# One semaphore of spent tiles in place of four bank counts behind the subtraction of row maxima

## What is computed

```python
# third attention (number 2 in the kernel): causal mask
scores = einsum('bhtd,bhsd->bhts', q, k) / sqrt(8) + causal
out = x + (softmax(scores) @ v) @ Wo.T + bo
# fourth attention (number 3): +1 outside a band of 16, then keep the 64 largest
scores = einsum('bhqd,bhkd->bhqk', q, k) * 8 ** -0.5 + outside
scores = where(scores >= kth, scores, 0)   # there are 64 keys, so all are kept
```

## Time and profile before

| | |
|---|---|
| median of 3 runs | 866.23 us |
| profiled execution | 868.9 us, its span (first to last instruction) 867.1 us |
| TensorE clock granted | 0.996 of full |
| TensorE matmul busy | 828.4 us (96%) in 7204 |
| VectorE busy | 630.4 us (73%) in 1587 |
| ScalarE busy | 567.4 us (65%) in 1569 |
| GpSimd busy | 286.4 us (33%) in 586 |
| attention 2, tiles 2 to 15 | 633 to 697 us |
| attention 3, tiles 0 to 15 | 745 to 833 us |

### The profile page before, as it was taken

How to read it: one execution, slowest core, us unless ns; L and a number is a source line. 1 busy time by engine, 2 the same in 40 slices (tenths; PEclk the granted TensorE clock), 3 DMA queues, 4 the chain that set the end, 5 groups by cost and what they waited for, 6 DMA issues and landing times.

```text
span 867.1 us, 20115 instructions
## 1 busy us (share of the span) xinstructions
PE 828.4 (96%) x7204; PEld 571.1 (66%) x7204; DVE 630.4 (73%) x1587; ACT 567.4 (65%) x1569; POOL 286.4 (33%) x586
## 2 busy tenths in 40 slices
PE   9999999999999999999999999999999989899986
PEld 8887888888889976544444444444467665676652
DVE  5677776777776655685785766775989876789876
ACT  3666677677777676866545586445477779677664
POOL 4355444444554442200000000002156520334355
PEclk9999999999999999999999999999999999999999
DMA  8700000000000000000000000000000000000000
GB/s 340 156 2 2 1 2 1 2 2 1 2 1 2 2 1 2 1 1 0 1 0 1 0 1 0 1 0 1 1 27 3 4 3 1 2 4 3 3 15 37
DMA packets 7821, 13.55 MB, mean 16 GB/s; under 512 B 4342, under 2 KB 5036, under 8 KB 7468
## 3 DMA queue, kind: packets, MB, share of 16 engines
q1 hardware_dynamic: 7724, 12.27, 4.5%
HBM read 11.22 MB, written 1.05 MB: 14 GB/s over the span
## 4 chain that ended last, share of the span: by engine, by line
PE 59%; DVE 20%; POOL 10%; issue 6%; ACT 4%; DMA 0%; DVEq 0%; POOLq 0%; SPq 0%; ACTq 0%
PE psum L1551 10%; PE psum L767 6%; POOL rstd L515 4%; PE psum L807 4%; DVE arena L2083 3%; PE psum L750 3%; PE psum L759 3%; POOL arena L1095 2%; DVE negmax L1005 2%; PE psum L835 2%; PE psum L1560 2%; PE psum L1978 2%; ACT arena L905 2%; PE psum L2367 2%; PE psum L1570 2%
## 5 line engine op out<-in xcount | busy, mean ns | idle before, releaser
L512 POOL TENSOR_TENSOR ve<-mv,epsv 128x1 f32<-128x1 f32 x176 | 36.3, 206 | 462.1 <-DVE mv L507 462.1
L1551 PE MATMUL psum<-arena,w1f 128*128 128x512 f32 x240 | 109.5, 592 | 0.0
L515 POOL TENSOR_TENSOR rstd<-ve,epsv 128x1 f32<-128x1 f32 x176 | 101.2, 575 | 13.8
L905 ACT ACTIVATE arena<-psum,negmax 128x128 f32<-128x128 f32 x256 | 90.5, 407 | 22.2 <-DVE negmax L1005 22.2
L1551 PEld LDWEIGHTS psum<-arena,w1f 128*128 128x128 f32 x240 | 45.5, 190 | 49.9 <-issue 46.1
L1095 POOL TENSOR_TENSOR arena<-arena,rsum 128x512 f32<-128x512 f32 x64 | 65.2, 1039 | 5.6 <-DVE rsum L1011 5.6
L905 ACT ACTIVATION_READ_ACCUMULATOR arena<-psum,negmax 128x1 f32 x256 | 63.2, 247 | 0.0
L1005 DVE TENSOR_REDUCE negmax<-psum 128x8 f32<-128x1024 f32 x32 | 39.2, 1225 | 32.9 <-PE psum L807 32.9
L750 PE MATMUL psum<-arena,sclA 128*128 128x128 f32 x512 | 62.5, 275 | 0.1
L767 PE MATMUL psum<-arena 128*128 128x512 f32 x128 | 61.2, 598 | 0.7 <-DVE arena L1000 0.4
L807 PE MATMUL psum<-arena 128*128 128x128 f32 x512 | 59.9, 275 | 0.0
(11 more groups left out here) (371 smaller groups left out, 1995.7 us busy)
## 6 DMA issues: line engine op xcount, KB each, us to landing
w<-in_w0qk SPq DMA_DIRECT2D x2, 512.0 KB, 4.6
w<-in_w0vo SPq DMA_DIRECT2D x1, 1024.0 KB, 7.3
cT<-in_cT SPq DMA_DIRECT2D x1, 1024.0 KB, 16.7
out<-x_tok SPq DMA_DIRECT2D x4, 256.0 KB, 2.2
rows<-in_rows SPq DMA_DIRECT2D x1, 836.0 KB, 12.3
x_tok<-in_x_tok SPq DMA_DIRECT2D x1, 768.0 KB, 9.4
ctx_tok<-in_ctx_tok SPq DMA_DIRECT2D x1, 768.0 KB, 10.8
wa<-in_wa SPq DMA_DIRECT2D x1, 768.0 KB, 18.5
```

The costliest lines, as they stand in the source:

```text
L515: pool.tensor_tensor(rstd[:, u, self.i:self.i + 1], ve[:, u, self.i:self.i + 1], epsv[:, 1:2], ALU.pow) \
L905: m = nc.scalar.activation(e0[:, b, g, :], ps(k, P, j * P), ACT.Exp, bias=negmax0[:, b, g:g + 1], accum_out=sum0[:, b, g:g + 1])
L1551: nc.tensor.matmul(ps(k), w1("e2", j * 384 + arg * D, j * 384 + (arg + 1) * D), f1_Hm[:, n, 2 * j + i, :], start=False, stop=False)
```

## The change

Each of the two attentions gets one semaphore `spent`, which the subtraction raises on completion. TensorE's four mask matmuls wait for `spent >= t` instead of each for its own bank (tile 0 still waits for the banks, which other jobs held before). ScalarE's exponential has one wait in place of four. VectorE's wait and three increments behind each subtraction go; at tile 15 VectorE waits once and raises all four banks by 16, so that the plan's counts hold for the jobs behind.

```diff
-            spread, maxed, exped, inverted = (sem(f"a{n}_{x}") for x in ("spread", "max", "exp", "rsum"))
+            spread, maxed, exped, inverted, spent = (sem(f"a{n}_{x}") for x in ("spread", "max", "exp", "rsum", "spent"))
...
-                        fill(pe, a, f"s{i}", t)
+                        if t.n == 0:
+                            fill(pe, a, f"s{i}", t)
+                        else:
+                            pe.wait_ge(spent, t.n)
...
-                    for i in range(4):
-                        stored(act, a, f"s{i}", t)
+                    act.wait_ge(spent, t.times(1, 1))
...
-                        .then_inc(free[0], 1)
-                    stored(dve, a, "s0", t)
-                    for i in range(1, 4):
-                        dve.sem_inc(free[i], 1)
+                        .then_inc(spent, 1)
+                    if t.n == TILES - 1:
+                        dve.wait_ge(spent, TILES)
+                        for i in range(4):
+                            dve.sem_inc(free[i], TILES)
```

## The result

The changed kernel takes 863.4 us (median of 20 runs, 860.44 to 866.58) against 866.76 us (20 runs, 865.67 to 868.94) for the kernel before, measured beside each other: ratio 0.9956, interval 0.9946 to 0.9966. Measured again in a pair of 8 and 27 runs it gave 863.66 against 867.77, ratio 0.9940 (0.9917 to 0.9963). The forecast was 861.6 us, in a range of 859.6 to 865.0, and faster. (Of the partner runs of the kernel before, one took 949.4 us at a granted clock of 0.85; it is left out everywhere.)

The account below looks back on a forecast made before the run. No engine's busy share decides: attention 2 loops through TensorE, attention 3 through VectorE's gap, barely above a TensorE-ScalarE cycle. Terms 0.4 + 2.2 + 1.05 + 1.2 - 0.2 = 4.65 us, from 866.23 to 861.6; range 859.6 to 865.0.

Parts of the forecast that it names:

- the forecast's own case: Whole kernel: gain of 3.3 to 5.9 us, time 860.3 to 862.9 us; chance 0.56.
- the first rival: Attention 3: the other cycle, TensorE with ScalarE, already bounds it; gain only 2.4 us, time 863.8; chance 0.22.
- VectorE's gap, 0.41 us a tile: Behind each subtraction: removing wait and increments saves VectorE 0.33 us idle plus 0.09 overlap, about 0.41 a tile.
- Masks, 0.54 to 0.39: TensorE's four mask matmuls, released together by one signal, take 0.39 instead of 0.54 us: 0.15 a held tile.
- Attention 2, 2.2 forecast: Tiles 2 to 15: ten loops gain 0.15 us, three gain 0.25 as TensorE becomes their bound at 4.69: 2.2 us.
- Attention 3, up to the first gate: Four loops give 0.25 us, held masks 0.15, VectorE's lead paid out at the gate 0.65: sum 1.05 us.
- to the second gate: Attention 3, between the gates: VectorE saves five gaps, paid out against TensorE's stands of 0.34 and 1.01: 1.2 us.
- Tile 15: Last tile of each attention: VectorE still waits, then issues four increments instead of three; loss 0.1 us each.
- the ring of 5.00 us: Attention 3: TensorE and ScalarE have a cycle of their own at 5.00 us, against VectorE's step of about 5.07.
- More than the sum: Whole kernel: all bounds at their upper end, gain 5.9 us and pauses of issue, time 859.9; chance 0.08.
- The change does not do what it says: VectorE's next instruction still held, first mask released as now; masks alone give under 1 us, about 865.8; chance 0.10.
- the slower case: Attention 3: GpSimd's second root grows by 0.27 us beside a gapless VectorE, 4.3 us in 16 tiles, 868.1; chance 0.04.

Follow-up runs that it names:

- the signal alone: Changed kernel, but VectorE keeps a wait and three increments, on a semaphore nobody waits for, behind each subtraction: 869.45 us, ratio 1.0015.
- L521 out of the way: L521 moved behind the next step's maxima in attention 2: 861.57 us on the changed kernel (ratio 0.9928), 868.27 on the kernel before (1.0015).
- the short product: GpSimd spreads one of eight key blocks from tile 2 of attention 2: 862.93 us on the changed kernel, 865.22 on the kernel before.
- the longer gap: Kernel before with three more increments, of a semaphore nobody waits for, behind VectorE's own after each subtraction: 871.48 us (one run).

## Why the prediction held, and where it didn't

The direction and the range held. The median of 863.4 us lies outside the forecast's own case, though (860.3 to 862.9), and is inside the whole range because that was widened for the first rival. The total by stretches (5.2 us against 4.65) is near the sum because two errors of opposite sign met, which is luck, and the median is further off because of a third.

**VectorE's gap, 0.41 us a tile: right.** The next instruction starts at 649.46, and the subtraction is recorded from 648.33 for 1.22, so 0.09 before its end: 0.33 of gap and 0.09 of overlap, as worked out from the earlier trace rows. In attention 3 the loops that stayed bound by VectorE fell from 5.07 to 4.64 (twice), 5.29 to 4.84, 7.85 to 7.43, 8.01 to 7.59 and 6.48 to 6.06 us: 0.42 to 0.45 each. The rule weighed in the prediction (the Trainium skill, VectorE: DVE Perf Modes, "The DRAIN you can't avoid") would have given 0.33 and semaphores that cost nothing. The traces speak against both parts for semaphore instructions that stand by themselves: three more cost 0.28 us. The same section of the page does add that a next instruction that isn't held starts earlier, which the prediction passed over, and the trace agrees with that (0.09 us).

**Masks, 0.54 to 0.39: right,** and worth less than 0.15 in every loop: 1.14 us in attention 2 and nothing in attention 3 up to the first gate, where 0.15 was forecast (the signal alone). Chain of waits of the kernel after, where the earlier trace rows had 0.54:

```profile
648.41 1.15 DVE arena L2085
649.55 0.05 issue
649.60 0.39 PE psum L1941 x4
...
654.50 0.27 ACT arena L2057
654.76 0.07 issue
654.83 1.04 POOL arena L2124
```

**Attention 2, 2.2 forecast, 1.42 measured: the term that was too large.** The step that failed is the one in which the loop bound by VectorE loses its 0.41 us and TensorE becomes its bound at 4.69. It took VectorE's instructions at their durations of before. The chain above shows the piece that it left out, GpSimd's spreading, and L521 beside it grew by up to 0.7 us. The piece could have been read. The loop of 4.95 us in the earlier trace rows was said to have no pause but the gap; it holds the L521 of 0.64 us shown above, 0.30 more than alone. (Five of the 13 loops were of this longer kind, not three.) A page of the Trainium skill bears on this (SBUF — State Buffer, "SBUF: two separate sides"): VectorE and GpSimd share a port pair, which a GpSimd instruction, or a VectorE one in a two-port mode or with two inputs in SBUF, locks for its whole length, and the other is blocked. The trace agrees in that the loser ended 0.08 us behind the winner; no run here shows which mode L521 was in. With L521 out of the way in both kernels the change gave 2.15 us, and with the short product in both 2.03, so without the hold-up the 2.2 forecast was nearly right. (The changed kernel with L521 moved lies 2.79 us below the kernel before, but 0.65 of that is the move.)

**Attention 3, up to the first gate: 1.05 forecast, 1.52 measured; to the second gate 1.2 and 1.64.** The place of the payment was wrong. I had VectorE's lead paid out at the gates, where TensorE stood 0.81 and 1.01 us, and little in between, as TensorE and ScalarE went round in 5.00 us. What was paid at a gate is one gap (0.42 each), where 0.65 was forecast at the first. The four loops in front of the first gate, forecast at 0.25 us together, gave 0.95: one of them a whole gap, the others 0.14 to 0.23 each, down to 4.81 and 4.93 us. The step that failed is taking 5.00 us for a ring of its own. Its exponential waited 0.45 us for the last increment; I counted nothing for that. The real ring was that of VectorE and GpSimd at 5.07, which the longer gap showed. Behind it lies TensorE's ring with ScalarE, which bounds two loops of the kernel after at 4.93 us. Its chain of waits:

```profile
761.86 0.33 PE psum L634
762.19 0.33 PE psum L1941 x4
762.51 0.62 PE psum L1951 x16
763.13 0.43 PE psum L2011 x2
...
764.13 0.59 ACT arena L2049
764.72 0.47 issue
765.19 0.30 ACT arena L2038
...
765.85 0.72 ACT arena L2418
766.57 0.17 ACT lnT L644
...
766.79 0.33 PE psum L634
```

No VectorE piece is in it. The two errors of attention 3 (0.5 and 0.4 us) and the 0.3 behind it have one sign, that of attention 2 (0.8) the other, and the sum came to 5.2 instead of 4.65 us.

**The stands at the gates** shrank as forecast: ahead of the fillers of the first gate no stand is recorded, the stand of 0.34 us for the add is gone too, and at the second the fillers begin 0.19 us behind L573 instead of 1.01.

```profile
801.91 0.94 PE L266 MATMUL psum<-const 128*128 128x128 f32 x6 [0.19 <-DVE x_tok L573]
```

**Behind the second gate** nothing was forecast and 0.3 came: the loop of tile 12 to 13 fell from 6.48 to 6.06, one gap. That TensorE isn't held by the subtraction there didn't mean that VectorE wasn't on the path.

**Tile 15:** the cost was forecast at 0.1 us each. At the end it is 0.15; between the attentions the stretch varies from 45.4 to 46.0 us with and without the change even where the clock isn't lowered, so the other can't be read. VectorE's next work begins 0.41 us behind the subtraction, with four increments on the chain (the first is shown):

```profile
696.43 1.23 DVE arena L2085
697.66 0.03 issue
697.68 0.02 DVEq L2091
697.71 0.07 issue
...
698.07 0.06 DVE arena L2095
```

**ScalarE** was counted at nothing. Its stands for the subtraction fell from 8.8 us in 10 places to 3.9 in 6, and the signal alone, which has all of this, gave nothing in attention 3. So counting nothing for the release was right, though the wait itself was evidence against the ring of 5.00 us.

**The rivals.** "The other cycle holds" (863.8) lies close to the measured median by number, not by mechanism: its 2.4 us stand against 5.2 by stretches. By stretches the gain lies between the sum and "More than the sum" (5.9). "The change does not do what it says" is out: VectorE's next instruction starts ahead of the subtraction's recorded end, and the gain is not the masks' alone. GpSimd's roots did not grow (no more of them at 0.82 us in attention 3 than before, busy time 286.6 against 286.4 us), so nothing spoke for the slower case. What holds the median at 863.4, above the forecast, although the stretches gave more than the sum, is a step of the prediction that I hadn't seen as one: it took the median of the changed kernel to lie as far below its profiled execution as before (2.7 us), thus at the clock of before. It lay 0.8 us above it (863.4 against 862.58). The clock was 0.9975 in the median of the 66 runs of the kernel before, and 0.995 after.

## What to carry to other kernels

A wait and a few increments on a compute engine cost that engine time of its own (here 0.09 us for an increment, and 0.41 for the wait and three increments with the lost overlap), and are worth removing where the chain runs through them. An experiment that adds more of them prices every stretch at once, but look whether another instruction became shorter by it, as L521 did here. Before a ring of two engines is taken as a floor, look at what each waits for inside it: a 0.45 us wait for the engine that is about to get faster means that it isn't one. And when an engine gets earlier, ask which instruction of its neighbour it now runs beside.

## What the runs showed of the hardware

- A semaphore increment by itself takes 0.09 us of VectorE's time (three more: idle time 0.33 to 0.61 us), and a wait for the instruction just ahead forgoes an overlap of 0.09 us.
- Four waits on one semaphore that is raised once release four matmuls together: 0.39 us for the masks, as when nothing holds them.
- A VectorE tensor-scalar in fp32, from SBUF to SBUF, of 0.34 us alone took 0.86 and 1.05 us beside a GpSimd product of 1.04 us, and ended 0.08 us behind it. A VectorE instruction reading PSUM was not lengthened by the same product (kernel before: L2105, from 649.74, 0.28 us, inside GpSimd's 649.43 to 650.47).
- A fall of the granted clock to its lower level (1.2 GHz) came, in 7 of 13 profiles that have it, behind a stand of TensorE of 0.76 us, and what followed was then up to 1.5 us later; 0.001 of mean clock went with 0.6 to 0.7 us of an execution, by the fits to the runs of the two kernels. Where the median of a kernel is compared with another's within 0.5%, the clocks have to be compared first.
